# A Swin block and an FFT-gated convolution block on one core: three images in work instead of two, softmax sums on TensorE, norms on ScalarE, and every engine's order rewritten

## The chip, the cores and the metric

The kernel runs on 1 core of one Trainium2 chip. Its time is device time in microseconds (us). Before the change it is 1808.63 us, the median of 3 runs (1806.32 to 1815.72).

## What is computed

The input is `x`, 16 images of 128 channels by 32 x 32 pixels, all in fp32. Each image goes through two blocks in turn.

The first is a Swin block over 16 windows of 8 x 8 tokens, with 8 heads of 16 channels:

```python
t = ln(tok, ln1_g, ln1_b)                      # in windows of 64 tokens
q, k, v = split(t @ qkv_w.T + qkv_b)
attn = softmax(q * 16**-0.5 @ k.T + bias)      # per window and head, 64 x 64
tok = tok + (attn @ v) @ proj_w.T + proj_b
tok = tok + gelu(ln(tok, ln2_g, ln2_b) @ w1.T + b1) @ w2.T + b2
```

The second is a convolution block:

```python
out0 = gelu(conv1x1(x, in_w, in_b))
x_fca = abs(ifft2(fft2(out0) * x_att))         # = |x_att| * |out0|
xs = x_att2 * x_fca                            # x_att, x_att2: per-channel factors from means
x_sca = abs(ifft2(conv(xs, fgm_w1) * fft2(conv(xs, fgm_w2)) * (1 + boost * mask))) * alpha + xs * beta
h_out, v_out = two 7-tap dilated axis convolutions of out0, each then a 3x3 depthwise one
pyr = 3x3 depthwise of four grouped 3x3 convolutions of out0 with dilations 1, 6, 12, 20
edge = sigmoid(3x3 convolution of out0 to one channel)
out = conv1x1(relu(x + c0*(1+edge)*h_out + c1*(1+edge)*v_out + c2*(1-0.3*edge)*pyr + c3*point + c4*x_sca))
```

## The kernel before

Each of the five engines has one instruction stream written out by hand, and semaphores join them. TensorE, VectorE, ScalarE and GpSimd each run `swin_rest(0)` (on GpSimd `swin_only`), then `both(n, i)` fifteen times, with n the image in the convolution block and i = n + 1 the image in the Swin block, and last `conv_only(15)`. In `both` the work of the two images is interleaved by hand. In each stream it has three stretches.

- The front: the input is put in window order (`to_windows`, L1324), turned to tokens by TensorE (`x_transposes`, L473) and copied (`x_copy`). VectorE takes the first norm's statistics and applies the norm with eight `tensor_scalar` (`norm1`, L938, through `normalise`, L929). TensorE turns the result back and makes keys, queries and values (`queries_keys` L486, `v` L497). VectorE adds the bias of the keys (L949), and SyncE spreads them over `k_heads` with eight DMAs (`spread_keys`, L428), for which the first `scores` waits (`kh_dma`). Beside it runs the head of the convolution block of image n: `in_conv` (L602), its gelu (L1407), channel means and factors (L999 to L1026), and the first half of the four dilated convolutions (`pyramid`, L657, matmul at L674).
- Eight slots, one for each pair of windows j. `scores` (L518) goes into bank 2 or 3, VectorE adds the bias (L957) and takes the row maximum (L960), GpSimd subtracts it (`less_max`, L1666), ScalarE takes the exponential (L1382), VectorE sums the rows and inverts the sums (L964, L966), GpSimd widens the inverses (`widen_inverse`, L1677), TensorE turns the exponentials (L529), ScalarE copies them (L1387), and `values` (L540) multiplies them with v. After four pairs each, `spread_inverse` (L551) turns the inverses and VectorE multiplies with them (L972). The spectrum of the convolution block is laid through the slots by `conv_early` and `conv_late` on TensorE and ScalarE, and by `conv_slot` on VectorE, with 9 of the 18 taps of the depthwise convolutions (`taps`, L1088 and L1090). A tap is one VectorE pass over 128 x 1024 values.
- The tail: projection, residual and second norm (`residual_stats` L974, `norm2` L984), the MLP (`mlp`, L565: eight `up` matmuls, eight gelus, two `down` groups), and on VectorE the last 9 taps, then `gate_axes`, `add_magnitude`, `mixture` (L1143 to L1159) and `swin_out` (L988). Then ScalarE's `rectify` and TensorE's `out_conv` (L755) end image n.

GpSimd also makes the two axis convolutions (`axis_conv`, L1684), `resT` (L1660), `mix_pyramid` (L1718) and `square_sum` (L1725). `xs` is kept turned, so that `mirrored` (L1028) reads rows of the image in its inner loop. The sum over the nine shifted edge planes is a matmul with ones (`edge_spread`, L637).

Of the kernel before, what the change touches and what calls it, by code (L numbers as in the profile page):

```python
# [48 lines left out]
RUN = 31 * S1 + SIDE  # L49
# [6 lines left out]
def layout(*entries):  # L56
# [21 lines left out]
    ("even", P), ("odd0", P), ("odd", P), ("idft_h", P), ("high", CH), ("iota", 2))  # L78


def shape_constants():
# [41 lines left out]
    idft = diag(unpack, unpack, unpack, unpack).reshape(P, 4, n)  # L123
    put("idft_h", idft.transpose(0, 2, 1).reshape(P, P))
# [12 lines left out]
    put("iota", np.stack([np.arange(P), np.arange(P) + P], 1))  # L137
    return c.astype(np.float32)


def swin_conv_kernel(nc, x, cols, rows, mats, cons, rel_index, out):
    with ExitStack() as ctx:
# [46 lines left out]
        attn_out = xw  # L189
        xT = sb("xT", CH, C)  # L190
        x1T = xT
# [3 lines left out]
        qC, kC = sb("qC", TOK), sb("kC", TOK)  # L195
        k_heads = sb("k_heads", HEADS, WIN, WT)
# [4 lines left out]
        stats, mv = sb("stats", CH, 6), sb("mv", CH, 2)  # L201
        std, rstd = sb("std", CH), sb("rstd", CH)
        row_max, row_sum, row_inv = sb("row_max", 3, HEADS), sb("row_sum", 3, HEADS), sb("row_inv", PAIRS, HEADS)
        inv_wide = sb("inv_wide", PAIRS, HEADS, HD)
# [9 lines left out]
        fa, fb, fc, fd, xe, xo = (fft[:, k] for k in range(6))  # L214
        hidden = fft[:, 2:6]
# [3 lines left out]
        z_run = sb("z_run", 32 * S1)  # L219
        z_grid = z_run.rearrange("p (h w) -> p h w", w=S1)  # L220
        z_dram = nc.dram_tensor("z_dram", (9, GRID1), F32, kind="Internal")
        axis_part = sb("axis_part", SIDE, SIDE)
# [38 lines left out]
        ln1_std = sem("ln1_std")  # L261
        nT_sb = sem("nT_sb")
# [12 lines left out]
        s_max = sem("s_max")  # L275
        s_sub = sem("s_sub")
        s_exp = sem("s_exp")
        s_inv = sem("s_inv")
        iv_wide = sem("iv_wide")
        iv_ps = sem("iv_ps")  # L280
# [4 lines left out]
        o_sb = sem("o_sb")  # L285
# [3 lines left out]
        ln2_std = sem("ln2_std")  # L289
        n2T_sb = sem("n2T_sb")  # L290
# [25 lines left out]
        eb_ps = sem("eb_ps")  # L316
# [38 lines left out]
        mag_sb = sem("mag_sb")  # L355
        hv_sb = sem("hv_sb")
# [17 lines left out]
        xs_hw = xs.rearrange("p (w h) -> p h w", w=SIDE)  # L374
# [5 lines left out]
        SLOT_TAPS = (0, 0, 0, 2, 4, 4, 5, 7, 9)  # L380
# [3 lines left out]
        def _(sp):  # L384
# [52 lines left out]
            with sp.Fori(0, IMAGES - 2) as n:  # L437
                load(n + 2)
                spread_edge(n)
                spread_keys(n + 1)  # L440
                stack_pyramid(n)
                store(n)
# [11 lines left out]
        def _(pe):  # L454
# [110 lines left out]
            def mlp(i):  # L565
# [25 lines left out]
                for t in range(3):  # L591
                    up(t)
# [1250 lines left out]
```

## Time and profile before

| | |
|---|---|
| median of 3 runs | 1808.63 us |
| the profiled execution | 1805.41 us, its span 1803.6 us |
| span, `both` of one image | 106.6 to 109.7 us, in the mean about 108.3 |
| TensorE, mean granted clock | 0.953 of full speed |
| DMA share | small: 33 GB/s in the mean |

The busy shares of the engines stand in the rows below. An engine's busy share is an average over the three stretches. What the change is worth is read from which engine each stretch waits for. In the rows of the profile, x counts records; every fp32 matmul of the program leaves two, a transpose one. L numbers are lines of the kernel before.

### The profile page before, as it was taken

Reading aid. Unit: us, or ns where it says so; the run is one execution under the profiler, and the core shown is the slowest. Engines: PE = TensorE matmul, PEld = TensorE weight load, DVE = VectorE, ACT = ScalarE, POOL = GpSimd, SP = SyncE. Lnnn points to the kernel's source line nnn. Section 1 sums busy time; section 2 is a strip of 40 time slices with the busy share of each in tenths; the row PEclk is TensorE's granted clock in tenths of the full one; section 3 lists DMA queues with packets and bytes.
Section 4 is the critical chain, followed back from the end, with each engine's and each line's share of the span. In section 5 each row is a group of like instructions: output and inputs, shape, how many; then the busy total and the mean of one; then the engine's idle time right before and its main releaser. Section 6 shows DMA issues by size and latency. Waiting matters only on the chain.

```text
span 1803.6 us, 32142 instructions
## 1 busy us (share of the span) xinstructions
PE 1549.4 (86%) x11664; PEld 906.3 (50%) x11664; DVE 1364.0 (76%) x2455; ACT 864.2 (48%) x1380; POOL 684.9 (38%) x603
## 2 busy tenths in 40 slices
PE   5789899888989889888998988889888898988884
PEld 3346455464555546445463554546455464555542
DVE  4558778687777878788687777868788786778866
ACT  2344545455454544545455454544545545454533
POOL 3244251634416244251534416134251623416151
PEclk9899999999999999999999999999999999999997
DMA  4011020111102011020111102011020201102020
GB/s 147 1 26 41 26 52 1 43 33 37 39 23 53 0 37 39 25 51 0 43 33 37 39 23 53 0 37 39 25 51 0 58 18 37 39 12 53 0 54 12
DMA packets 19618, 60.23 MB, mean 33 GB/s; under 512 B 6228, under 2 KB 6228, under 8 KB 19204
## 3 DMA queue, kind: packets, MB, share of 16 engines
q1 hardware_dynamic: 19588, 59.83, 13.7%
q8 instruction: 18, 0.29, 0.1%
q14 instruction: 12, 0.10, 0.0%
HBM read 14.04 MB, written 9.02 MB: 13 GB/s over the span
## 4 chain that ended last, share of the span: by engine, by line
DVE 39%; PE 25%; DVEq 16%; issue 7%; ACT 6%; SPq 4%; DMA 3%; ACTq 1%; POOL 0%; POOLq 0%
DVE hv L1090 16%; DVEq L959 7%; DVE nT L929 5%; PE bank L647 5%; PE bank L674 4%; SPq L428 4%; DVE row_max L960 4%; DVEq L965 3%; PE bank L467 3%; PE bank L518 3%; PE bank L489 2%; DMA k_heads<-kC 2%; PE bank L755 2%; DVE score L957 2%; PE bank L577 1%
## 5 line engine op out<-in xcount | busy, mean ns | idle before, releaser
L674 PE MATMUL bank<-act,mats_sb 128*32 128x512 f32 (+11 forms) x2112 | 267.1, 475 | 1.4 <-DVE xs L1026 1.4
L1666 POOL TENSOR_TENSOR score<-score,row_max 128x512 f32<-128x512 f32 x128 | 133.4, 1042 | 306.7 <-DVE row_max L960 305.1
L1350 ACT ACTIVATE fft<-bank 128x512 f32<-128x512 f32 x224 | 168.9, 807 | 125.7 <-PE bank L467 111.8
L1090 DVE SCALAR_TENSOR_TENSOR hv<-hor,mix,hv 128x1024 f32<-128x1024 f32 x128 | 193.8, 1514 | 10.7
L467 PE MATMUL bank<-cons_sb,fft 128*128 128x128 f32 x1280 | 185.4, 306 | 11.8 <-DVE fft L1117 11.8
L1090 DVE SCALAR_TENSOR_TENSOR hv<-ver,mix,hv 128x1024 f32<-128x1024 f32 x144 | 186.9, 1298 | 11.0
L1382 ACT ACTIVATE score<-score 128x512 f32<-128x512 f32 x128 | 80.8, 631 | 225.8 <-POOL score L1666 225.8
L467 PEld LDWEIGHTS bank<-cons_sb,fft 128*128 128x128 f32 x1280 | 172.7, 217 | 31.4 <-DVE fft L1117 17.0
L1677 POOL COPY inv_wide<-row_inv 128x128 f32<-128x128 f32 x128 | 91.8, 717 | 206.7 <-DVE row_inv L966 206.7
L674 PEld LDWEIGHTS bank<-act,mats_sb 128*32 128x32 f32 x2112 | 117.5, 109 | 99.6 <-issue 81.5
L1696 POOL TENSOR_SCALAR hor<-act,cols_sb 128x1024 f32<-128x1024 f32 x16 | 18.0, 1125 | 391.6 <-ACT act L1407 391.6
L518 PE MATMUL bank<-k_heads,qC 128*64 128x512 f32 x512 | 136.1, 621 | 31.8 <-DMA k_heads<-kC 31.8
L577 PE MATMUL bank<-nC,mats_sb 128*128 128x512 f32 x256 | 127.4, 621 | 38.9 <-ACT nC L1350 23.4
L957 DVE TENSOR_TENSOR score<-bank,rel_bias 128x512 f32<-128x512 f32 x128 | 87.2, 681 | 76.3 <-PE bank L518 76.2
L1387 ACT ACTIVATE probT<-bank 128x512 f32<-128x512 f32 x128 | 77.7, 607 | 101.6 <-PE bank L529 101.3
L1706 POOL TENSOR_SCALAR axis_part<-act,cols_sb 128x320 f32<-128x320 f32 (+1 forms) x128 | 109.4, 855 | 22.5 <-issue 22.5
L587 PE MATMUL bank<-fft,mats_sb 128*128 128x512 f32 x256 | 115.2, 593 | 0.0
L1400 ACT ACTIVATE fft<-bank,fold_b 128x512 f32<-128x512 f32 x128 | 79.2, 689 | 68.5 <-PE bank L577 68.5
L929 DVE TENSOR_SCALAR nT<-xT,mv,rstd 128x128 f32<-128x128 f32 x256 | 104.8, 491 | 3.8
L1708 POOL TENSOR_TENSOR ver<-ver,axis_part 128x320 f32<-128x320 f32 (+1 forms) x64 | 100.8, 1575 | 9.4
L960 DVE TENSOR_REDUCE row_max<-score 128x8 f32<-128x512 f32 x128 | 87.8, 686 | 11.6
L577 PEld LDWEIGHTS bank<-nC,mats_sb 128*128 128x128 f32 x256 | 45.1, 191 | 98.2 <-issue 34.4
(180 smaller groups left out, 2903.9 us busy)
## 6 DMA issues: line engine op xcount, KB each, us to landing
pyr_stack<-pyr SPq DMA_DIRECT2D x192, 144.2 KB, 3.1
x_in<-x_dram SPq DMA_DIRECT2D x16, 512.0 KB, 3.5
k_heads<-kC SPq DMA_DIRECT2D x128, 64.0 KB, 2.4
out_dram<-y_out SPq DMA_DIRECT2D x16, 512.0 KB, 2.8
k_heads<-rel_dram SPq DMA_DIRECT2D x2, 1024.0 KB, 13.0
mats_sb<-mats_dram SPq DMA_DIRECT2D x1, 1978.5 KB, 7.4
z_dram<-z_sb SPq DMA_DIRECT2D x32, 19.1 KB
z_run<-z_dram SPq DMA_DIRECT2D x16, 38.2 KB
```

What stands on the lines that cost most here:

```text
L467: last = pe.matmul(dst[:, c * P:(c + 1) * P], src[:, at:at + P], rhs, start=True, stop=True)
L518: last = pe.matmul(bank[2 + j % 2][64 * e:64 * e + 64, :], qC[:, w * WT:(w + 1) * WT], k_heads[:, :, w], start=True, stop=True)
L577: pe.matmul(bank[b][:], w_up[:, f * P:(f + 1) * P], nC[:, HALF * k:HALF * k + HALF], start=True, stop=True).then_inc(up_ps, 1)
L587: last = pe.matmul(bank[b][:], w_down[:, f * P:(f + 1) * P], hidden[:, f, HALF * k:HALF * k + HALF], start=False, stop=(f == FC - 1))
L674: last = pe.matmul(grids[32 * d:32 * d + 32, y0 - 16 * k:y1 - 16 * k, x0:x1], w_pyr[:, d, t], act[:, y0 + dy:y1 + dy, x0 + dx:x1 + dx], st ...
L929: last = dve.tensor_scalar(nT[:, c], source[:, c], mv[:, c, 0:1], rstd[:, c:c + 1], ALU.subtract, ALU.mult)
L957: dve.tensor_tensor(score[:, j % 3].rearrange("p h k -> p (h k)"), bank[2 + j % 2][:], rel_bias[:], ALU.add).then_inc(s_biased, 1)
L959: dve.drain()
L960: dve.tensor_reduce(row_max[:, j % 3], score[:, j % 3], AX.X, ALU.max).then_inc(s_max, 1)
L1090: last = dve.scalar_tensor_tensor(hv[:], src, mix[:, a, k:k + 1], hv[:], ALU.mult, ALU.add)
L1350: return act_.activation(dst, src, ACT.Copy)
L1666: pool.tensor_tensor(score[:, j % 3], score[:, j % 3], row_max[:, j % 3].unsqueeze(2).broadcast_to([P, HEADS, WT]), ALU.subtract)\
```

## The change

In words, part by part:

1. Three images are in work. `both(n, i, f, late)` convolves image n, does attention and MLP of i = n + 1, and does the front of f = n + 2 (turns, norm 1, keys, queries, values) inside the slots 6 and 7 and inside the MLP of i. The end of image late = n - 1 (`gate_axes`, `add_magnitude`, `mixture`, `rectify`, `out_conv`) is moved to the start of `both`.
2. Softmax: `row_sums`, `widen_inverse` and `spread_inverse` go. `values` adds four matmuls for each pair of windows with a constant `pair`, which sum the exponentials; VectorE inverts 128 x 128 sums from PSUM and multiplies, once for each pair. The subtraction of the maximum moves from GpSimd to VectorE. All scores go through bank 2, one at a time.
3. Norms: VectorE computes 1/std and -mean/std, ScalarE applies them, eight activations for each norm. The keys' bias, `swin_out` and the first tap move from VectorE to ScalarE.
4. Spectrum: `xs` is kept in natural order and unscaled; the factor goes into `w1_scaled` and `w2_scaled` (128 x 128). `mirrored` makes only the 17 distinct rows, and `part_products` multiplies them in 64 matmuls with 32-column weights in place of 16 with 128.
5. `mix_pyramid` and `square_sum` move from GpSimd to VectorE. The edge sum leaves TensorE: three DMAs bring nine planes in rows, VectorE sums them, ScalarE takes the tanh of 32 x 32 values, and two DMAs through DRAM spread it over 128 partitions.
6. The taps: one on ScalarE in slot 2, one on VectorE in slot 6, one after `norm2(i, 0)`, two after the statistics of image f, thirteen at the very end. On TensorE, `conv_early` stands ahead of `scores` in a slot, and `pyramid_conv` is moved behind the slots.

The core of the diff (TensorE, VectorE, ScalarE; a line of "..." marks what is left out):

```diff
             def values(i, j):
                 pe.wait_ge(pT_sb, 8 * i + j + 1)
-                if j == 4:
-                    pe.wait_ge(o_sb, 2 * i + 1)
+                if j >= 2:
+                    pe.wait_ge(o_scaled, 8 * i + j - 1)
...
+                for g in range(HP):
+                    last = pe.matmul(ps[32 * g:32 * g + 32, P:2 * P], con("pair"),
+                                     probT[:, j % 2, g], start=True, stop=True)
                 last.then_inc(o_ps, 1)
...
+            def part_products(dst, parts, k):
+                for c in range(4):
+                    for q in range(4):
+                        a, r = divmod(4 * (4 * k + c) + q, 2)
+                        at = SIDE * (r if a == 0 else a + 1)
+                        last = pe.matmul(dst[32 * q:32 * q + 32, c * P:(c + 1) * P], parts[:, at:at + SIDE],
+                                         w1_scaled[:], start=True, stop=True)
+                return last
...
+            def both(n, i, f, late):
+                scores(i, 0)
+                in_conv(n, i + 1)
+                scores(i, 1)
                 edge_products(n)
                 pyramid(n, 0, range(0, 2))
                 gap_products(n)
+                pyramid(n, 0, range(2, 6))
                 mid_products(n)
+                pyramid(n, 0, range(6, 9))
                 for j in range(PAIRS):
+                    conv_early(n, j)
                     if j + 2 < PAIRS:
                         scores(i, j + 2)
                     prob_transposes(i, j)
+                    if j == 0 and late is not None:
+                        pe.wait_ge(z_copied, n + 1)
+                        pe.wait_ge(xs_sb, 2 * n + 1)
+                        out_conv(late)
                     conv_late(n, j)
+                    if j == 6 and f is not None:
+                        next_turns(i, f, 0)
+                    elif j == 7:
+                        project(i, 0, f)
                     values(i, j)
+                if f is not None:
+                    next_turns(i, f, 1)
                 last_odd(n)
                 project(i, 1)
+                pyramid_conv(n, 0)
                 n2_transposes(i, 0)
+                pyramid_conv(n, 1)
+                n2_transposes(i, 1)
+                mlp(i, n, f)
...
+                for t in range(6):
+                    up(i, t)
+                down(i, 0)
+                half_of(turn, 0)
+                half_of(turn, 1)
+                up(i, 6)
+                half_of(key, 0)
+                half_of(key, 1)
+                up(i, 7)
+                half_of(query, 0)
+                half_of(query, 1)
+                half_of(value, 0)
+                half_of(value, 1)
+                down(i, 1)
...
+            def scale_values(i, j):
+                dve.wait_ge(o_ps, 8 * i + j + 1)
+                ps = bank[(1, 3)[j % 2]]
+                dve.reciprocal(inverse[:, j % 2], ps[:, P:2 * P])
+                dve.drain()
+                dve.tensor_tensor(attn_out[:, P * j:P * j + P], ps[:, 0:P], inverse[:, j % 2], ALU.mult)\
+                   .then_inc(o_scaled, 1)
...
+            def both(n, i, f, late):
+                if late is not None:
+                    gate_axes(late)
+                    add_magnitude(late)
+                bias_max(i, 0)
                 gap(n)
+                bias_max(i, 1)
                 attention_vectors(n)
+                if late is not None:
+                    mixture(late)
                 scaled_input(n)
                 even_part(n)
                 route_logits(n)
                 for j in range(PAIRS):
+                    if j in (4, 5):
+                        conv_slot(n, j)
+                    if j > 0:
+                        scale_values(i, j - 1)
...
+                if f is not None:
+                    norm1_stats(f, 0)
+                scale_values(i, 7)
                 residual_stats(i, 0)
                 norm2(i, 0)
+                taps(n, range(SLOT_TAPS[PAIRS], SLOT_TAPS[PAIRS + 1]))
                 residual_stats(i, 1)
                 norm2(i, 1)
+                square_sum(n)
+                if f is not None:
+                    norm1_stats(f, 1)
+                taps(n, range(SLOT_TAPS[PAIRS + 1], SLOT_TAPS[PAIRS + 2]))
+                if f is not None:
+                    norm1(f)
+                gate_pyramid(n)
+                mix_pyramid(n)
+                taps(n, range(SLOT_TAPS[PAIRS + 2], 18))
```

Here `SLOT_TAPS` is (1, 1, 1, 1, 1, 1, 1, 2, 2, 3, 5), where it was (0, 0, 0, 2, 4, 4, 5, 7, 9).

## Rows read from the trace of the kernel before

**Rows 1.** The page: busy time by engine, dilated convolutions, keys' DMAs (last: us to landing).
```profile
PE 1549.4 (86%) x11664; PEld 906.3 (50%) x11664; DVE 1364.0 (76%) x2455; ACT 864.2 (48%) x1380; POOL 684.9 (38%) x603
L674 PE MATMUL bank<-act,mats_sb 128*32 128x512 f32 (+11 forms) x2112 | 267.1, 475 | 1.4 <-DVE xs L1026 1.4
...
k_heads<-kC SPq DMA_DIRECT2D x128, 64.0 KB, 2.4
```
**Rows 2.** Busy time by stretch: three images, the first Swin part, the last convolution.
```profile
core 0: us, PE busy (x) PEld busy (x) DVE busy (x) ACT busy (x) POOL busy (x), PEclk, DMA share, GB/s
751.90:1076.10 324.20, 285.98 (x2167) 167.26 (x2166) 252.97 (x453) 161.01 (x260) 125.82 (x111) 0.96 0.14 32
...
38.30:99.30 61.00, 43.42 (x334) 23.47 (x333) 25.94 (x64) 26.33 (x44) 10.32 (x16) 0.86 0.06 10
1724.50:1803.60 79.10, 49.16 (x361) 29.76 (x359) 52.89 (x58) 27.04 (x38) 29.03 (x20) 0.85 0.14 37
```
**Rows 3.** The same view in steps of 5 us, where the granted clock is low.
```profile
875.00:880.00 5.00, 5.00 (x13) 1.88 (x13) 3.51 (x5) 0.78 (x2) 4.68 (x4) 0.59 0.15 22
...
920.00:925.00 5.00, 4.68 (x19) 3.66 (x19) 4.65 (x7) 3.64 (x5) 2.15 (x2) 0.50 0.00 0
```
**Rows 4.** TensorE in order of time: start, us, line, x [idle before <-releaser].
```profile
873.34 3.78 PE L489 MATMUL bank<-nC,mats_sb 128*128 128x512 f32 x4
...
886.61 4.42 PE L674 MATMUL bank<-act,mats_sb 128*32 128x512 f32 x40
...
899.62 0.43 PE L540 MATMUL bank<-probT,v_pair 128*32 128x64 f32 x16
899.98 1.08 PE L518 MATMUL bank<-k_heads,qC 128*64 128x512 f32 x4
...
904.22 1.09 PE L459 MATMUL bank<-cons_sb,fft 128*128 128x128 f32 x8 [0.74 <-ACT fft L1350]
...
958.40 1.88 PE L577 MATMUL bank<-nC,mats_sb 128*128 128x512 f32 x4
```
**Rows 5.** Groups of TensorE by line and form, 751.9 to 1076.1 us.
```profile
L467 PE MATMUL bank<-mats_sb,fft 128*128 128x128 f32 x96 | 12.2, 280 | 3.8 <-DVE fft L1099 3.8
L551 PE MATMUL bank<-cons_sb,inv_wide 128*128 128x128 f32 x48 | 6.6, 281 | 0.0
L637 PE MATMUL bank<-z_run,ones 9*128 9x512 f32 x12 | 6.2, 634 | 3.0 <-DVE fft L1113 3.0
```
**Rows 6.** Groups of VectorE, the same three images.
```profile
L929 DVE TENSOR_SCALAR nT<-xT,mv,rstd 128x128 f32<-128x128 f32 x48 | 19.5, 473 | 0.7
L957 DVE TENSOR_TENSOR score<-bank,rel_bias 128x512 f32<-128x512 f32 x24 | 16.4, 681 | 11.8 <-PE bank L518 11.8
L964 DVE TENSOR_REDUCE row_sum<-score 128x8 f32<-128x512 f32 x24 | 16.2, 677 | 0.0
L1032 DVE TENSOR_TENSOR fft<-xs 128x930 f32<-128x930 f32 x6 | 14.1, 2342 | 0.3
```
**Rows 7.** Two lines of VectorE reciprocals over the run: ns least/median/most; 4, 8 values.
```profile
L926 DVE RECIPROCAL rstd<-std x48: 165/178/205, 23.4 to 1702.8; 128x4 f32<-128x4 f32 x32, 128x8 f32<-128x8 f32 x16
L966 DVE RECIPROCAL row_inv<-row_sum x128: 202/203/205, 51.7 to 1691.1; 128x8 f32<-128x8 f32 x128
```
**Rows 8.** VectorE in order of time, one image's tail.
```profile
936.90 4.42 DVE L1090 SCALAR_TENSOR_TENSOR hv<-hor,mix,hv 128x1024 f32<-128x1024 f32 x2
...
945.16 0.69 DVE L978 TENSOR_TENSOR xT<-bank,resT 128x512 f32<-128x512 f32 x1
...
946.89 0.38 DVE L921 BATCH_NORM_AGGREGATE mv<-stats 128x2 f32<-128x6 f32 x4
...
949.10 12.16 DVE L1090 SCALAR_TENSOR_TENSOR hv<-ver,mix,hv 128x1024 f32<-128x1024 f32 x9
```
**Rows 9.** GpSimd in order of time, beside the first row of Rows 8.
```profile
936.52 2.36 POOL L1718 TENSOR_TENSOR py<-py,xm 128x1024 f32<-128x1024 f32 x1
```
**Rows 10.** SyncE's queue in order of time: one image's spreading of the keys.
```profile
877.94 5.02 SPq L428 DMA_DIRECT2D k_heads<-kC  x8
```
**Rows 11.** A ScalarE group of small activations, the same three images.
```profile
L1329 ACT ACTIVATE xw<-x_in 128x256 f32<-128x256 f32 x14 | 4.7, 404 | 0.0
```

More of the change, by code:

```diff
@@ L508, in scores, with v @@
+            def v(i, k, b):
+                wv = w_qkv[:, 2 * C:3 * C].rearrange("p (g e d) -> p e g d", g=HP, e=2)
+                for w in range(8):
+                    t = nC1[:, (8 * k + w) * WT:(8 * k + w + 1) * WT]
+                    for e in range(2):
+                        last = pe.matmul(bank[b][64 * e:64 * e + 64, w * 64:w * 64 + 64], t, wv[:, e],
+                                         start=True, stop=True)
+                last.then_inc(v_ps, 1)
             def scores(i, j):
@@ new lines, in down @@
+            def down(i, k):
+                b = (0, 3)[k]
+                pe.wait_ge(up_sb, 8 * i + 4 + 4 * k)
+                for c in range(4):
+                    pe.matmul(bank[b][:, c * P:(c + 1) * P], x1T[:, 4 * k + c], ident, is_transpose=True,
+                              start=(c == 0), stop=False)
+                for f in range(FC):
+                    last = pe.matmul(bank[b][:], w_down[:, f * P:(f + 1) * P],
+                                     hidden[:, f, HALF * k:HALF * k + HALF], start=False, stop=(f == FC - 1))
+                last.then_inc(down_ps, 1)
@@ L760, in conv_early @@
                 if j == 1:
-                    pyramid(n, 1, range(6, 9))
+                    pyramid(n, 1, range(4, 9))
                 elif j == 2:
@@ L848, in conv_only @@
                 mid_products(n)
-                pyramid(n, 1, range(0, 5))
+                pe.wait_ge(z_copied, n + 1)
+                pe.wait_ge(xs_sb, 2 * n + 1)
+                out_conv(n - 1)
                 for j in range(PAIRS):
@@ L853, in conv_only @@
                 last_odd(n)
+                pyramid_conv(n, 0)
+                pyramid_conv(n, 1)
+                for k in range(2):
+                    pe.wait_ge(py_sb, 2 * n + k + 1)
                 out_conv(n)
@@ L1235, in conv_only @@
                     conv_slot(n, j)
-                    if j == 3:
-                        r_even_bias(n)
+                    taps(n, range(SLOT_TAPS[j], SLOT_TAPS[j + 1]))
                 taps(n, range(SLOT_TAPS[PAIRS], 18))
+                square_sum(n)
+                gate_pyramid(n)
+                mix_pyramid(n)
                 gate_axes(n)
```

828 lines of the change are left out of this document (401 added, 427 removed).

## The prediction, made before the changed kernel ran

> **What bounds the kernel now.** I read the busy shares first. TensorE is busy 86% of the span, VectorE 76%, the others under half [rows 1]. Over three images in the steady state that is 95.3 us of TensorE and 84.3 us of VectorE in a period of about 108.1 us [rows 2]. So neither is the bound alone: 12.8 us of each period TensorE has nothing to do. Then the clock: in two places of each image it falls to the lower of its two levels (1.2 of 2.4 GHz), after stretches in which TensorE had waited for the norms and for VectorE's half of the spectrum [rows 3]. Four records of 512 columns then take 3.78 us, against 1.88 us at full clock [rows 4]. Over both places I put this at about 5 us of the 95.3. Last the order of time: the tail has nine taps in a row on VectorE, 12.16 us [rows 8], and only behind them come the passes that free `rectify` and `out_conv`. The next image's front then runs as one long chain (turn, statistics, norm, turn, keys, DMA), in which the keys' DMAs alone take 5.02 us of issue and 2.4 us of landing [rows 1, 10].
>
> So the period is a ring through several engines. What the change brings is the shortest ring that is left, not the sum of what it removes.
>
> **TensorE's work.** Removed: `edge_spread`, 6.2 us in three images, 2.1 each, and `spread_inverse`, 6.6, 2.2 each [rows 5]. For what is added I need the price of matmuls with 32-column weights. The 40 records at 886.61 are steps 0 to 4 of `pyramid`, each step four matmuls into four partition groups. By the shapes in the code their longest members have 512, 496, 512, 496, 496 columns, 2512 together, for 4.42 us [rows 4]: 1.7 ns for each column of the longest, the other three free. `values` agrees: two steps of 64 columns, 0.36 us from its start to the next one's [rows 4]. The sums by `pair` are one such step of 128 columns for each of 8 pairs: 8 x 0.21 = 1.7 us. Were the four one after another, it would be 0.43 each, 3.5 us. `part_products` is 16 steps of 128 columns, 3.5 us, in place of 96 records in three images, 12.2 us, 4.1 each [rows 5]; one after another it would be 14. The sum is -2.1 - 2.2 + 1.7 - 0.6 = -3.2 us, up to +9 if nothing runs side by side. I take -3.2, the nearest rows being of the same form. With the clock kept, TensorE needs about 87 us.
>
> **VectorE's work.** Removed for each image: applying the norms, 19.5/3 = 6.5 us; row sums 5.4 [rows 6] and their inverses 8 x 0.2 = 1.6 [rows 7]; keys' bias, `scale_values`, first tap and `swin_out`, about 5.4 by the same kind of passes. `mirrored` handles 465 values where it had 930, at 2342 ns twice [rows 6]: -2.4. `xs` unscaled and in natural order: about -2. In sum -23. Added: subtracting the maximum, a pass like L957's at 0.68 us [rows 6], 8 x 0.69 = 5.5; `mix_pyramid` and `square_sum` 2.5; the edge sum, small vectors and inverses 1.2; and 8 times a reciprocal of 128 x 128 and a product. No row shows a reciprocal of that width. Four values take 165 to 178 ns, eight 203 [rows 7], so 6.3 to 9.5 ns a value: 0.96 to 1.34 us, and 0.28 if the width cost as little as in a sum. I take 1.1, with 0.3 for the product 8 x 1.4 = 11.2. VectorE ends near 84.3 - 23 + 20.4 = 82 us, hardly less than before, with about 5 us of drains between the passes. The gain can't come from VectorE being relieved.
>
> The Trainium skill (VectorE: DVE Perf Modes, First, the fixed hardware budget) says that Reciprocal repeats its divide step 8 times. That is the same direction as the slope in the rows; it gives no other sum.
>
> **The ring after the change.** I call D the moment when VectorE starts the bias of `scores(i, 0)`, V the end of `values(i, 7)` on TensorE.
>
> D to V is TensorE's: since all scores share bank 2, `scores(i, 1)` waits for that first bias, 0.8 us. Then at full clock: seven `scores` at 1.0, 7.1; eight groups of four turns at 0.5 (eight turns: 1.09 [rows 4]), 4.0; `pyramid` 267.1/16 = 16.7 [rows 1]; `values` with the sums 8 x 0.57 = 4.6; five products of the spectrum at 16 records x 0.127 = 2.0, the columns 2.0 and both `part_products`, 15.7; the turns of the spectrum, of x and `project`, 4.0; the late `out_conv` 1.9; edge and vector products 1.5. Together 55.5, so V at D + 56.3. To this come waits for ScalarE's copies, 0.74 us at a time [rows 4], since `conv_early` now stands ahead of the `scores` that covered them, and some low clock after D: I add 4.2. V at D + 60.5.
>
> V to the next D is VectorE's: the last `scale_values` with its wait 1.7; `residual_stats` twice, 945.16 to the end of the aggregates at 947.27, 2.1 each [rows 8], 4.2; the two roots and inverses 1.9; `square_sum` 1.3; statistics of image f 1.4; inverses 0.4; `gate_pyramid` and `mix_pyramid` 2.9; and 1 + 2 + 13 taps at 12.16/9 = 1.35 [rows 8], 21.6; then `gate_axes` and `add_magnitude` of the late image 2.7. Together 38.1. TensorE needs less in the same stretch: last products and `pyramid_conv` 8.7, the wait for the second norm 2, eight `up` 7.2 and two `down` 8.0 (0.9 us a matmul of 512 columns [rows 4]), the front of f 6.5, together about 33; the keys' DMAs are hidden behind queries, values and `down(1)`. The ScalarE part (sixteen norm activations at under 0.4 us [rows 11], keys, `swin_out`) lies within it.
>
> To this comes what GpSimd takes from VectorE. At 936.90 two taps take 4.42 us, not 2.7, while a GpSimd pass of 2.36 us runs [rows 8, 9]: VectorE stands until that pass is over. In the new tail `resT` falls among VectorE's passes (1.2), and `axis_conv` starts with `gate_axes` and `add_magnitude` (1.7): 41.0. The period is 60.5 + 41.0 = 101.5 us, against 108.3.
>
> **The total.** The first Swin part ends at 38.3 + 61.0 = 99.3 us [rows 2]; it gets the front of image 1, and loses GpSimd's steps: the first D at 104. Fifteen periods, 1522.5, less 5 because the last has no image f. From the last D to the end, now 79.1 us for the whole of `conv_only` [rows 2]: less 7 (half mirrors, one tap, GpSimd's two slow passes), plus 2.6 for the late image's passes: 74.5. The sum is 104 + 1522.5 - 5 + 74.5 = 1696 us of span. The profiled execution lies 1.8 above its span, and the median of the runs 3.2 above the profiled execution: 1700 us.
>
> **The rivals.**
> 1. The waits, the low clock and GpSimd's share come out at almost nothing. The ring is then 56.3 + 38.1 = 94.4, with one or two us left 96: 104 + 1440 + 69.5 = 1614 us (69.5 is 74.5 - 5), 1619 measured. For it: the new order has far fewer chains of several engines, and TensorE alone needs 87. Against it: VectorE's tail must leave TensorE idle for some 5 us each image, and such gaps cost clock before.
> 2. The gain is given back in the slots. One bank for `scores` and `conv_early` at the head make each slot wait for a copy and a bias: 8 slots x 0.74 us [rows 4] more than I have, period 107.4, 1785 to 1790 us. Against it: VectorE is ahead of TensorE in the slots by about 5 us in my timeline.
> 3. Slower: GpSimd and VectorE stand in each other's way on the ring. GpSimd's `axis_conv` and `resT` (125.8/3 = 41.9 us [rows 2] less its steps for the softmax and its two passes, about 19) now come in one block behind D, where VectorE has about 16 passes that GpSimd can hold up. I have priced these at 9 us in all. If each pays what the tap at 936.90 paid, 4.42 - 2.7 = 1.7 us [rows 8], it is 27, 18 more; about 5 is slack, so the period is 114.5: 104 + 1717.5 + 69.5 = 1891, 1896 measured. It decides from 12 us more than I have. For it: every pass of this stretch stands ahead of what TensorE waits for (`mid_products`, `out_conv`). Against it: GpSimd ran under VectorE before as well, and its group L929 there lost only part of its time [rows 6].
>
> The Trainium skill (SBUF — State Buffer, Who interferes with whom) says that a VectorE instruction with two SBUF inputs and a GpSimd one that reads SBUF exclude each other for their whole length. By that rule rival 3 has its mechanism, and the trace agrees at 936.90; how often they meet, it doesn't say.
>
> That the change doesn't do what it says is in rival 2: the front is moved, but its time comes back as waits.
>
> **How the numbers follow.** Forecast 0.64 (ring 98 to 105.5, 1645 to 1760 us), rival 1 0.14, rival 2 0.12, rival 3 0.10. The range takes in the forecast, the upper half of rival 1 and rival 2's lower part: 1625 to 1785, leaving out about 0.2. The reciprocal's bounds move the period by under 2 us (one lies in the tail, eight use up slack), the packed matmuls' upper bound by 12. Two measurements of this kernel differ by up to about 0.5%, 9 us: faster by more 0.86, within it 0.04, slower 0.10.
>
> **What would show it.** Period by the stores near 101.5 us. VectorE's thirteen taps in a row, some 17.6 us, and TensorE waiting 3 to 6 us at `scores(i, 1)` for VectorE: right. TensorE waiting for the keys' DMA instead: the tail is not VectorE's. The reciprocal of 128 x 128 near 1.1 us; the `pair` group near 0.2 us a pair; `part_products` near 1.75 us a call. Taps and subtractions well over 1.28 and 0.7 us in the first 25 us behind D, with TensorE idle at `mid_products`: rival 3. Idle ahead of each slot's first group: rival 2. It is all wrong if TensorE is never idle ahead of `scores(i, 1)`: then my ring is not the one that closes last.

## The result and the profile after

The changed kernel takes 1600.93 us, the median of 4 runs (1598.29 to 1607.63), beside 1812.18 us for the kernel before on the same chip. The ratio is 0.884, with a 95% interval from 0.880 to 0.888: 11.6% faster. The forecast was 1700 us and its range ended at 1625; the time lies 24 us below it, and 18 us below the 1619 of rival 1. The sign was right, the size was not.

The page of the kernel after, its span, its busy shares and its row of the TensorE clock in 40 slices:

```profile
span 1600.2 us, 36298 instructions
PE 1453.8 (91%) x13904; PEld 843.6 (53%) x13904; DVE 1287.5 (80%) x2311; ACT 942.7 (59%) x1685; POOL 376.6 (24%) x315
PEclk9889999999999999999999999999999999999987
```

Three images of its steady state, as [rows 2] shows them for the kernel before (stretch, its length, the busy time of each engine with its records, granted clock, DMA share, GB/s):

```profile
783.60:1067.40 283.80, 268.03 (x2595) 156.10 (x2587) 240.12 (x427) 175.31 (x316) 68.81 (x58) 0.99 0.17 42
```

For each image TensorE is busy 89.3 us (95.3 before), VectorE 80.0 (84.3), GpSimd 22.9 (41.9). TensorE's idle time has gone from 12.8 us to 5.3. The stores of the images lie 94.5 us apart in the mean of 13 intervals, where the kernel before had 108.1 (14 intervals) and the forecast was 101.5. So neither engine was relieved by much. Of the 13.5 us between the two windows, 7.5 is idle time of TensorE that is gone, 6.0 its busy time.

TensorE from one D to the stretch behind it. Columns: start, duration, engine, line, operation, output and inputs, records, and in brackets the idle time before it and who ended it.

```profile
862.07 1.08 PE L530 MATMUL bank<-k_heads,qC 128*64 128x512 f32 x4 [2.87 <-DVE score L1013]
863.94 3.52 PE L703 MATMUL bank<-act,mats_sb 128*32 128x512 f32 x12
867.77 3.42 PE L703 MATMUL bank<-act,mats_sb 128*32 128x480 f32 x26
875.90 1.88 PE L795 MATMUL bank<-fft,mats_sb 128*128 128x512 f32 x4
...
894.37 0.40 PE L557 MATMUL bank<-probT,cons_sb 128*32 128x128 f32 x8
894.59 1.93 PE L734 MATMUL bank<-w_scaled,fft 128*32 128x128 f32 x64
...
918.80 0.40 PE L557 MATMUL bank<-probT,cons_sb 128*32 128x128 f32 x8
...
951.37 1.08 PE L530 MATMUL bank<-k_heads,qC 128*64 128x512 f32 x4
952.38 1.98 PE L652 MATMUL bank<-xm,mats_sb 128*128 128x512 f32 x4
957.23 1.08 PE L530 MATMUL bank<-k_heads,qC 128*64 128x512 f32 x4 [2.87 <-DVE score L1013]
```

The first record is `scores(i, 1)`, and it waits 2.87 us for VectorE's first bias, as does the last, one image later. `scores(i, 0)` and `in_conv` of that next image (951.37, 952.38) are done well before: the keys' DMAs, which had 5.02 us of issue on the path [rows 10], are out of it. V is 919.20, the end of the last `pair` sums. An image without low clock behind the same wait, and the granted clock at both places (columns as above):

```profile
768.63 1.08 PE L530 MATMUL bank<-k_heads,qC 128*64 128x512 f32 x4 [2.87 <-DVE score L1013]
780.76 1.88 PE L795 MATMUL bank<-fft,mats_sb 128*128 128x512 f32 x4
```

```profile
768.60:773.60 5.00, 4.97 (x45) 2.08 (x48) 4.30 (x10) 2.75 (x4) 4.37 (x5) 1.00 0.04 8
862.10:867.10 5.00, 5.00 (x22) 1.17 (x22) 3.58 (x6) 1.96 (x3) 4.37 (x5) 0.66 0.04 7
```

VectorE from V to the next D:

```profile
919.27 0.96 DVE L1026 RECIPROCAL inverse<-bank 128x128 f32<-128x128 f32 x1 [0.88 <-PE bank L557]
920.51 0.68 DVE L1036 TENSOR_TENSOR x1T<-bank,resT 128x512 f32<-128x512 f32 x1
930.42 2.65 DVE L1144 SCALAR_TENSOR_TENSOR hv<-hor,mix,hv 128x1024 f32<-128x1024 f32 x2
936.19 5.36 DVE L1144 SCALAR_TENSOR_TENSOR hv<-hor,mix,hv 128x1024 f32<-128x1024 f32 x4
941.62 12.16 DVE L1144 SCALAR_TENSOR_TENSOR hv<-ver,mix,hv 128x1024 f32<-128x1024 f32 x9
955.29 1.28 DVE L1215 SCALAR_TENSOR_TENSOR hv<-fft,mix,hv 128x1024 f32<-128x1024 f32 x1
956.50 0.68 DVE L1013 TENSOR_TENSOR score<-bank,rel_bias 128x512 f32<-128x512 f32 x1
```

But for two waits of 0.37 and 0.36 us for ScalarE's roots it works on to the next bias at 956.50. So the ring of the forecast is there: V to D on VectorE is 37.3 us, in the other images 37.2 to 37.5 (forecast 41.0). D to V on TensorE is 861.34 to 919.20, 57.9 us, in this image (forecast 60.5). The image at 768.63 has the same wait and takes 56.2, since the clock stays at its upper level there. Of the 14 images from D = 201.90 on, seven have the full clock and 56.2 us, seven the low one and 57.7 to 57.9, one of these 59.1. In the mean over all fifteen, D to V is 57.0, and the period from D to D is 94.3. The sum of the bare terms had been 94.4.

### The profile page after: what moved, and what is told of

Same layout as the page of the kernel before. It is cut to its first block, busy times and chain, and to the rows that moved or that the text cites. A ratio compares the mean times of both kernels' runs of the same rounds, so it can differ in the third digit from the quotient of the medians.

```text
span 1600.2 us, 36298 instructions
## 1 busy us (share of the span) xinstructions
PE 1453.8 (91%) x13904; PEld 843.6 (53%) x13904; DVE 1287.5 (80%) x2311; ACT 942.7 (59%) x1685; POOL 376.6 (24%) x315
## 4 chain that ended last, share of the span: by engine, by line
DVE 39%; PE 28%; DVEq 16%; ACT 10%; issue 6%; DMA 1%; SPq 0%; ACTq 0%
DVE hv L1144 17%; PE bank L703 15%; ACT fft L1444 4%; DVEq L1015 4%; PE bank L530 3%; DVE row_max L1016 3%; DVEq L1027 3%; DVE stats L984 2%; PE bank L795 2%; ACT probT L1487 2%; DVEq L1039 2%; DVE score L1018 2%; DVEq L985 2%; DVE score L1013 1%; PE bank L673 1%
## 5 line engine op out<-in xcount | busy, mean ns | idle before, releaser
L703 PE MATMUL bank<-act,mats_sb 128*32 128x512 f32 (+11 forms) x2112 | 280.0, 492 | 0.0
L1806 POOL TENSOR_TENSOR resT<-qC,proj_shift 128x1024 f32<-128x1024 f32 x16 | 38.0, 2377 | 622.6 <-DVE x1T L1036 618.0
L703 PEld LDWEIGHTS bank<-act,mats_sb 128*32 128x32 f32 x2112 | 121.6, 113 | 104.7 <-issue 83.0
L1144 DVE SCALAR_TENSOR_TENSOR hv<-hor,mix,hv 128x1024 f32<-128x1024 f32 x128 | 164.4, 1284 | 10.6
L1444 ACT ACTIVATE fft<-bank 128x512 f32<-128x512 f32 x224 | 165.4, 810 | 12.8 <-PE bank L489 11.6
L489 PE MATMUL bank<-cons_sb,fft 128*128 128x128 f32 x1280 | 162.0, 280 | 7.8 <-DVE fft L1177 7.2
L1013 DVE TENSOR_TENSOR score<-bank,rel_bias 128x512 f32<-128x512 f32 x128 | 87.4, 682 | 96.9 <-PE bank L530 96.9
L489 PEld LDWEIGHTS bank<-cons_sb,fft 128*128 128x128 f32 x1280 | 148.8, 192 | 20.8 <-DVE fft L1177 10.8
L1026 DVE RECIPROCAL inverse<-bank 128x128 f32<-128x128 f32 x128 | 122.0, 953 | 44.2 <-PE bank L557 44.2
L1018 DVE TENSOR_TENSOR score<-score,row_max 128x512 f32<-128x512 f32 x128 | 98.8, 772 | 10.0 <-issue 0.5
L541 PEld LDWEIGHTS bank<-cons_sb,score 128*128 128x128 f32 x512 | 55.7, 142 | 79.1 <-issue 66.1
L1016 DVE TENSOR_REDUCE row_max<-score 128x8 f32<-128x512 f32 x128 | 87.8, 686 | 11.7
L1838 POOL TENSOR_TENSOR hor<-hor,axis_part 128x320 f32<-128x320 f32 (+1 forms) x64 | 94.3, 1473 | 9.4 <-issue 0.2
L683 PE MATMUL bank<-pyr_stack,mats_sb 96*32 96x512 f32 x768 | 88.9, 596 | 0.0
```

Source lines behind the costliest of these rows:

```text
L489: last = pe.matmul(dst[:, c * P:(c + 1) * P], src[:, at:at + P], rhs, start=True, stop=True)
L703: last = pe.matmul(grids[32 * d:32 * d + 32, y0 - 16 * k:y1 - 16 * k, x0:x1], w_pyr[:, d, t], act[:, y0 + dy:y1 + dy, x0 + dx:x1 + dx], st ...
L1016: dve.tensor_reduce(row_max[:, j % 3], score[:, j % 3], AX.X, ALU.max)
L1018: dve.tensor_tensor(score[:, j % 3], score[:, j % 3], row_max[:, j % 3].unsqueeze(2).broadcast_to([P, HEADS, WT]), ALU.subtract)\
L1026: dve.reciprocal(inverse[:, j % 2], ps[:, P:2 * P])
L1144: last = dve.scalar_tensor_tensor(hv[:], src, mix[:, a, k:k + 1], hv[:], ALU.mult, ALU.add)
```

## The experiments

My theory, once the trace was read: the ring D, V, D is what sets the period; its bare sum was right, and the two allowances on top were too large (4.2 us for copies and low clock between D and V, 2.9 for GpSimd). The runs were made on several chips, on which the kernel before took 1811 to 1815 us; a difference of a few us counts only where the traces show it too, from D to D. Rivals: VectorE as a whole sets the time, so that any pass taken from it counts in full; or GpSimd's passes set it; or the gain comes from single parts (the norms on ScalarE) that would have brought it in the old order too.

**Two taps fewer in the tail.**

```diff
-                taps(n, range(SLOT_TAPS[PAIRS + 2], 18))
+                taps(n, range(7, 18))
```

> The changed kernel with two of the thirteen taps at the end of VectorE's tail left out (taps 5 and 6, so the output lacks them). Ring theory: the period is TensorE from D to V and VectorE from V to the next D, and TensorE stands 2.87 us ahead of scores(i, 1) in each image. Two taps are 2.7 us, so each of 15 periods falls by 2.7 us, from 94.5 to 91.8, the whole from 1601 to about 1560 us, and the wait ahead of scores(i, 1) shrinks to 0.2 us. Rival TensorE (busy 94% of the period, so it is the bound and VectorE is beside it): no change, 1595 to 1601. Rival VectorE's sum (busy 80 of 94.5): also 1560, told apart by the run with five taps less.

Measured: 1547.41 us (ratio 0.854, 0.850 to 0.859), 53 us less for 40 us of passes. More comes back than is taken out. Two images in a row:

```profile
927.13 0.68 DVE L1013 TENSOR_TENSOR score<-bank,rel_bias 128x512 f32<-128x512 f32 x1
1017.88 0.69 DVE L1013 TENSOR_TENSOR score<-bank,rel_bias 128x512 f32<-128x512 f32 x1
```

The last `pair` sums of this image start at 982.90 and take 0.40. So D to V is 56.2 us and V to D 34.6. The tail is shorter by the taps, 2.7, in every image, about 40 us in all. TensorE waits no more than 0.17 us at `scores(i, 1)`, the granted clock behind it is 1.00 in every image, and D to V is 56.2 in 11 of 15. That takes 1.7 us, once 3.0, from the seven images that had low clock behind the wait, 13 us together. 40 and 13 make up the 53. I had expected 1560: the clock was not in it. My own sum for D to V without allowance had been 56.3.

**Five taps fewer.**

```diff
-                taps(n, range(SLOT_TAPS[PAIRS + 2], 18))
+                taps(n, range(10, 18))
```

> The changed kernel with five taps of the thirteen left out (6.75 us). Ring theory: the ring closes through TensorE's own tail as soon as 2.9 us are gone, since scores(i, 1) stands behind in_conv there; period 91.6, total about 1557 us, nearly the same as with two taps less. Rival VectorE's sum: 6.75 x 15 = 101 us less, 1500. Rival TensorE: no change.

Measured: 1540.50 us (0.851, 0.846 to 0.855). Three more taps, 4 us an image, bring 7 us in all. VectorE alone would have brought 60 more; that rival is dead. Now VectorE waits at D for TensorE:

```profile
924.76 0.69 DVE L1013 TENSOR_TENSOR score<-bank,rel_bias 128x512 f32<-128x512 f32 x1 [2.71 <-PE bank L530]
1015.29 0.69 DVE L1013 TENSOR_TENSOR score<-bank,rel_bias 128x512 f32<-128x512 f32 x1 [2.72 <-PE bank L530]
```

The period is 90.5 us, TensorE's floor with this order. The expected 1557 was again 17 us too high.

**Two taps made twice.**

```diff
-                taps(n, range(SLOT_TAPS[PAIRS + 2], 18))
+                taps(n, (5, 6, *range(5, 18)))
```

> The changed kernel with two taps of the tail done twice (the output has them twice). Ring theory: period 94.5 + 2.7 = 97.2, total 1601 + 40 = 1641 us, the wait ahead of scores(i, 1) 5.6 us in place of 2.87; some more low clock behind it may add up to 1 us a period (1656). Rival TensorE: up to 2.9 us a period are free, 1601.

Measured: 1667.88 us (0.921, 0.916 to 0.925), 67 us more for 40 us of passes; I had expected up to 55.

```profile
899.60 1.97 PE L530 MATMUL bank<-k_heads,qC 128*64 128x512 f32 x4 [6.26 <-DVE score L1013]
998.62 1.98 PE L530 MATMUL bank<-k_heads,qC 128*64 128x512 f32 x4 [6.27 <-DVE score L1013]
...
996.00 1.97 DVE L1215 SCALAR_TENSOR_TENSOR hv<-fft,mix,hv 128x1024 f32<-128x1024 f32 x1
```

The period is 99.0. The wait has grown from 2.87 to 6.26 us, and `scores(i, 1)` takes 1.97 us where it took 1.08: the low clock now follows in every image but the first (0.50 to 0.56 in the 5 us behind the wait), and D to V is 58.3 where the mean was 57.0. The magnitude pass ahead of D takes 1.97 instead of 1.28, as it starts at 996.00 while GpSimd's first `axis_conv` pass, 2.20 us from 994.69, still runs. So of 4.7 us a period 2.7 are the taps, 1.3 the clock and 0.7 GpSimd's.

**Almost no axis convolution on GpSimd.**

```diff
-            OFFSETS = [0] + [AXIS_DIL * (t - mid) for t in range(AXIS_TAPS)
-                             if t != mid and abs(AXIS_DIL * (t - mid)) < SIDE]
+            OFFSETS = [0]
```

> The changed kernel with only the centre tap of both axis convolutions on GpSimd (the others left out, the output lacks them): GpSimd works 2.3 us there instead of about 20. Ring theory: VectorE loses about 5 us to GpSimd within the first 22 us behind D, but in a stretch where it later waits 3.7 us for scores(i, 3), so the period stays within 0.5 us, total 1593 to 1601. Contention theory (my rival 3 at a smaller size: that the hold-ups are on the ring): 3 to 5 us a period less, 1526 to 1556 us.

Measured: 1604.03 us (0.886, 0.880 to 0.892), the same as with all of it. The page of the profile counts GpSimd busy 99.4 us instead of 376.6, and nothing came of it:

```profile
961.90 1.08 PE L530 MATMUL bank<-k_heads,qC 128*64 128x512 f32 x4 [2.87 <-DVE score L1013]
```

The same wait of 2.87 us. What GpSimd takes from VectorE behind D falls into slack. Rival 3 has no room left.

**The biases ahead of the late image's passes.**

```diff
-                if late is not None:
-                    gate_axes(late)
-                    add_magnitude(late)
                 bias_max(i, 0)
                 gap(n)
+                if late is not None:
+                    gate_axes(late)
+                    add_magnitude(late)
                 bias_max(i, 1)
                 attention_vectors(n)
```

> The changed kernel with VectorE's order at the start of an image turned: bias and maximum of scores(i, 0) and the channel mean first, then gate_axes and add_magnitude of the late image (2.7 us). Nothing is left out. Ring theory: scores(i, 1) starts 2.7 us earlier, the wait of 2.87 us ahead of it falls to about 0.2, period 94.5 - 2.7 = 91.8, total 1601 - 38 = 1563 us. Rival: the two passes then stand ahead of the channel factors, TensorE waits at mid_products instead, and the period stays at 94 to 94.5 (1594 to 1601).

Measured: 1588.19 us (0.876, 0.874 to 0.878), 12.7 us less, where I had expected 38. The wait did not go, it moved:

```profile
863.75 0.38 PE L665 MATMUL bank<-vec,mats_sb 128*128 128x1 f32 x2 [1.94 <-DVE vec L1067]
956.45 0.38 PE L665 MATMUL bank<-vec,mats_sb 128*128 128x1 f32 x2 [1.95 <-DVE vec L1067]
```

TensorE now waits 1.94 us at `mid_products`, because the passes stand ahead of `attention_vectors`. V to D is 34.5 us, 2.8 less, but D to V is 58.2, and in five of 13 periods 59.8 to 60.8: there the granted clock from 10.7 us behind D to V is 0.97, in the others 1.00. My ring had one point of contact; there are two close together. The expectation failed on that, and on the clock.

**Both norms back on VectorE.**

```diff
+                dve.wait_ge(nT_ps, 2 * i)
                 invert(mv1, std1, rstd1, shift1, ln1_inv, slice(0, CH))
+                apply_norm(nT1, xT, mv1, rstd1, range(CH), nT_sb)
...
+                dve.wait_ge(n2T_ps, 2 * i)
                 invert(mv2, std2, rstd2, shift2, ln2_inv, slice(4 * k, 4 * k + 4))
+                apply_norm(nT, x1T, mv2, rstd2, range(4 * k, 4 * k + 4), n2T_sb)
```

`normalise1` and `normalise2` go from ScalarE.

> The changed kernel with both norms applied by VectorE again, sixteen passes over 128 x 128, and not by ScalarE: this undoes one part of the change. Before, four of them took 1.1 us without GpSimd beside them. Ring theory: all sixteen lie between V and the next D, 4.5 us more, period 99, total 1601 + 67 = 1668 us; the second norm reaches TensorE a little earlier, which helps nothing. Rival TensorE: 2.9 us of it free, about 1 us a period, 1616 us.

Measured: 1704.92 us (0.941, 0.938 to 0.943), 104 us more: half of the whole gain hangs on this part. The sixteen passes of one image in three groups, the D behind them, and the wait one image later (L993 and L1023 are lines of this kernel, the norm and the bias):

```profile
883.66 1.11 DVE L993 TENSOR_SCALAR nT<-x1T,mv,rstd 128x128 f32<-128x128 f32 x4
889.41 1.12 DVE L993 TENSOR_SCALAR nT<-x1T,mv,rstd 128x128 f32<-128x128 f32 x4
896.09 2.14 DVE L993 TENSOR_SCALAR nT<-qC,mv,rstd 128x128 f32<-128x128 f32 x8
922.08 0.68 DVE L1023 TENSOR_TENSOR score<-bank,rel_bias 128x512 f32<-128x512 f32 x1
...
1024.74 1.97 PE L530 MATMUL bank<-k_heads,qC 128*64 128x512 f32 x4 [5.88 <-DVE score L1023]
```

V is 879.4, so V to D is 42.7 us, 5.4 more than after the change: 4.4 are the passes, and 0.7 is the magnitude pass ahead of D, which takes 1.97 instead of 1.28 behind GpSimd's first, as with two taps more. D to V is 57.7 to 59.4, in the mean 58.6 instead of 57.0: with a wait of 5.88 us the low clock comes in every image but the first (0.70 to 0.85 in the 10 us behind it). The period is 101.3 in the mean. I had expected 1668: the 37 us on top are this clock and the 0.9 us by which V to D passed my 4.5.

**The same part alone, in the kernel before.** VectorE makes 1/std and -mean/std, ScalarE applies both norms, everything else as before:

```diff
             def norm1(i):
                 dve.wait_ge(ln1_std, i + 1)
-                dve.wait_ge(xT_sb, 2 * i + 2)
-                dve.wait_ge(n2T_ps, 2 * i)
-                normalise(xT, nT_sb)
+                invert(rstd1, shift1, ln1_inv)
...
                 deviation1(i)
+                normalise1(i)
                 n_copy(i)
```

> The kernel before with one part of the change alone: VectorE makes 1/std and -mean/std, ScalarE applies both norms. In the old order the norm stands on the chain to the keys: eight activations of 0.40 us (3.2) in place of passes that took 2.2 to 4.3, and one more hand-over; the second norm costs TensorE some 0.5 us twice, and VectorE's tail begins 2.2 us earlier. In sum between +1 and -2 us an image: 1805 us (1780 to 1825). Rival: what counts is the work that VectorE gives up, 5 to 6 us an image, as undoing the same part after the change cost 6.5 us and more: then 1720 us or less.

Measured: 1825.33 us, 1.008 of the kernel before (1.005 to 1.011): a little slower, at the upper end of what I expected. The rival's 1720 is refuted: the part is worth nothing by itself. TensorE at the first matmuls of the MLP, first in this kernel, then in the kernel before:

```profile
956.02 2.81 PE L581 MATMUL bank<-nC,mats_sb 128*128 128x512 f32 x6 [1.86 <-ACT nC L1366]
```

```profile
946.68 2.81 PE L577 MATMUL bank<-nC,mats_sb 128*128 128x512 f32 x6 [0.78 <-ACT nC L1350]
```

Over the whole run TensorE waits 40.9 us at this line for `nC`, against 23.4 in the kernel before. In the old order TensorE waits for the norm itself, and ScalarE is slower at it. In the new order the norm lies beside other work, and what counts is VectorE's length.

**Two taps fewer in the kernel before.**

```diff
-                taps(n, range(SLOT_TAPS[PAIRS], 18))
+                taps(n, range(SLOT_TAPS[PAIRS], 16))
```

The edit stands in `both` and in `conv_only`.

> The kernel before, with the last two of the eighteen taps left out (part of the computation is missing). Did the kernel before hang on VectorE's tail? In its trace TensorE waits 1.35 us at the output matmul for the end of that tail, while the MLP had ended just before. If that wait is all, the 2.7 us of the two taps bring 1.4 us an image and a little clock: 1785 us (1775 to 1795). Rival: VectorE's tail stands on the ring in full, as it does after the change, where two taps brought 3.6 us an image: then 1750 to 1765 us.

Measured: 1788.32 us (0.988, 0.985 to 0.991), 22.7 us less, as expected. The same edit brought 53 us after the change. What ended TensorE's idle time ahead of `out_conv` (L755), in the kernel before and in this one (us, times):

```profile
  ACT fft L1521: 37.3, 14
```

```profile
  ACT fft L1521: 17.0, 1
```

In the kernel before, 19.74 of the 37.3 us stand in the last image, the other 13 waits are 1.35 us each. With two taps fewer those 13 are gone. So before the change VectorE's tail stood on the path for 1.4 us an image at most; what stood behind it was the path.

**Two passes back on GpSimd.** `mix_pyramid` and `square_sum`, each with its waits, as in the kernel before:

```diff
-                square_sum(n)
                 if f is not None:
                     norm1_stats(f, 1)
...
                 gate_pyramid(n)
-                mix_pyramid(n)
```

> The changed kernel with mix_pyramid and square_sum on GpSimd again, each one pass of 2.35 us over 128 x 1024, instead of 1.23 on VectorE: this undoes another part. Both lie between V and the next D. Theory that the two engines exclude each other for whole passes: VectorE saves 2.5 us and loses up to 2.35 at each of the two (it stood that long at 936.90 before), so the period is 94.5 + 0 to 2.2, total 1601 to 1635 us. Theory that GpSimd's time is free: period 92, total 1565 us.

Measured: 1611.67 us (0.889, 0.886 to 0.892), 11 us more, although VectorE has 2.5 us less to do in each image. The interval touches that of the changed kernel (0.880 to 0.888), but the traces differ too, 95.1 us from D to D against 94.3. First GpSimd's two passes, then VectorE's taps beside them:

```profile
935.75 2.35 POOL L1844 TENSOR_TENSOR fft<-fft 128x1024 f32<-128x1024 f32 x1
942.59 3.25 POOL L1837 TENSOR_TENSOR py<-py,xm 128x1024 f32<-128x1024 f32 x1 [4.49 <-DVE py L1191]
...
937.14 3.40 DVE L1144 SCALAR_TENSOR_TENSOR hv<-hor,mix,hv 128x1024 f32<-128x1024 f32 x2
942.34 7.30 DVE L1144 SCALAR_TENSOR_TENSOR hv<-hor,mix,hv 128x1024 f32<-128x1024 f32 x4
```

Two taps take 3.40 us instead of 2.65, four take 7.30 instead of 5.36: 2.7 us of waiting for 2.5 us of work handed over. V to D is 37.55 us instead of 37.3, so nothing is saved, and 4 us in all are lost. The rest of the 11 is TensorE's clock: behind the wait, here 2.49 us, it is low in 12 of 14 images, where it was in 7, and D to V is 57.7 to 57.9 in them. Why it is so in more of them I can't say. A GpSimd pass of this kind runs in VectorE's time when VectorE has two-input passes to make. The Trainium skill (SBUF — State Buffer, Who interferes with whom) says that such pairs exclude each other; here the trace agrees, and the statistics at 935.73, which have one input, are not held up.

**A version built from these: three taps early.** The slots have slack on VectorE (it waits 3.67 us for `scores(3)` at 886.83), the tail has none. The first tap goes to slot 0 on ScalarE, two more stand in slot 1 ahead of the bias of `scores(3)`:

```diff
-        SLOT_TAPS = (1, 1, 1, 1, 1, 1, 1, 2, 2, 3, 5)
+        SLOT_TAPS = (3, 3, 3, 3, 3, 3, 3, 4, 4, 5, 7)
...
+                    if j == 1:
+                        taps(n, range(1, 3))
                     if j + 2 < PAIRS:
                         bias_max(i, j + 2)
```

> The changed kernel with the first tap (ScalarE) in slot 0 and taps 1 and 2 (VectorE) in slot 1 ahead of the bias of scores(i, 3), where VectorE waits 3.7 us for TensorE; eleven taps in the tail instead of thirteen. Nothing is left out. Ring theory: the same work, 2.7 us of it moved from the ring into slack: period 91.8 to 92.3, total 1560 to 1568 us, as with two taps left out. Theory that VectorE's sum counts: no change, 1595 to 1601.

Measured: 1547.47 us (4 runs; 0.854, 0.852 to 0.856): nothing left out, and as fast as with two taps fewer. TensorE at D, and four images of it:

```profile
928.92 1.08 PE L530 MATMUL bank<-k_heads,qC 128*64 128x512 f32 x4 [0.16 <-DVE score L1013]
930.40 2.22 PE L703 MATMUL bank<-act,mats_sb 128*32 128x512 f32 x12
941.05 1.88 PE L795 MATMUL bank<-fft,mats_sb 128*128 128x512 f32 x4
```

```profile
783.00:1147.00 364.00, 353.11 (x3456) 207.27 (x3459) 323.97 (x569) 233.29 (x421) 94.44 (x76) 1.00 0.18 43
```

The wait is 0.16 us, the clock full, TensorE busy 97%. From this `scores(i, 1)` to `out_conv` it is 12.13 us (928.92 to 941.05); after the change it was 13.83 (862.07 to 875.90), the same instructions and no wait of TensorE between them. The image at 768.63 took 12.13 as well, with the wait. So it is the low clock that costs 1.7 us, in the images that have it; here none has it. The run lies 13 us below the lower end of what I had expected; that share of the clock, 13 us, was not counted in it.

**And the last image.** On top of it, for `conv_only` alone (shown beside the changed kernel):

```diff
                 gap_products(n)
-                pyramid(n, 0, range(0, 9))
+                pyramid(n, 0, range(0, 4))
                 mid_products(n)
+                pyramid(n, 0, range(4, 9))
...
                 for j in range(PAIRS):
                     conv_slot(n, j)
-                    taps(n, range(SLOT_TAPS[j], SLOT_TAPS[j + 1]))
-                taps(n, range(SLOT_TAPS[PAIRS], 18))
+                    if j == 2:
+                        taps(n, range(1, 9))
+                taps(n, range(9, 18))
```

> The early taps of the run before, and two changes for the last image alone: TensorE makes the vector products behind step 4 of the pyramid instead of behind step 9, and VectorE makes the taps 1 to 8 right behind the third slot's work instead of behind the sixth's. In the run before, VectorE stood idle there for 6.97 us (for the vector products) and for 3.02 us (for the first product of the spectrum), while TensorE waited 15.79 us for VectorE at its end. If VectorE's work sets the end of the last image, nearly all of the 10 us comes back: 1538 us (1534 to 1542). Rival: TensorE's spectrum sets it, being started no earlier; then 1544 to 1548, no change.

Measured: 1541.12 us (4 runs; 0.852, 0.849 to 0.854), 6.3 us less than the run before it; that is 14.9% below the kernel before, and the fastest of all that compute everything. It was another chip, and the two intervals overlap, but from the last D of `both` to the end the traces have 156.2 us against 162.0. TensorE's idle time ahead of the last `out_conv` went from 15.79 us to 7.46:

```profile
1504.66 3.30 PE L734 MATMUL bank<-w_scaled,fft 128*32 128x128 f32 x64 [1.97 <-DVE fft L1153]
1530.77 3.75 PE L795 MATMUL bank<-fft,mats_sb 128*128 128x512 f32 x4 [7.46 <-ACT fft L1654]
```

I had counted on nearly all of 10 us. VectorE still waits 2.35 us for the vector products, and the group at 1504.66 now takes 3.30 us instead of 1.95, behind a wait.

## Why the prediction was wrong, point by point

- *What bounds the kernel, and the ring after the change.* Right. It is TensorE from D to V and VectorE from V to D, with `scores(i, 1)` waiting 2.87 us (said: 3 to 6, so just below). Taking time from VectorE's tail moves the period, taking it from GpSimd does not. The old kernel had no such ring: two taps are worth 22.7 us there and 53 here.
- *The bare sums.* Right, and that they hit within 0.1 us is partly luck. D to V was 56.3 us, measured 56.2 wherever the clock is full, 57.0 in the mean. V to D was 38.1; measured 37.3, of which about 0.4 is GpSimd's. So one sum was 0.7 short and the other 0.8 long, and 94.4 stands against 94.3.
- *The allowance of 4.2 us between D and V.* This step failed. It was put down in one line, "waits for ScalarE's copies, 0.74 us at a time" and some low clock, with no count of places. Measured is 57.0 - 56.3 = 0.7 us in the mean: nothing in one half of the images, 1.7 in the other. Between `scores(i, 1)` and V TensorE waits twice, 0.52 us for a copy of ScalarE's and 0.48 for VectorE, and the bare sum absorbed both; the rest is the low clock, 0.81 and 0.84 from 860 to 870 us.
- *The allowance of 2.9 us for GpSimd.* This step failed too. I had charged `resT` with 1.2 and the start of `axis_conv` with 1.7, by the tap of 4.42 us [rows 8]. After the change `resT` runs from 925.55, beside statistics and small vectors, and costs 0.4: L993 (there -mean/std) takes 0.55 us, not 0.16. At D it was GpSimd that gave way: its first pass takes 2.09 us instead of 1.12, VectorE's two passes their usual 1.23 and 1.28. VectorE's pass had started 0.20 us before it. In the kernel with two taps more GpSimd's pass was the one under way, and VectorE's took 1.97 us. The 9 us that rival 3 says were priced in all stand nowhere in the forecast's sum; it has these 2.9.
- *The size.* 15 periods came out 104.7 us shorter than forecast, and the ends 8.9 longer (the first D at 109.1, said 104; the last D to the end 78.3, said 74.5). In the first Swin part, with no convolution beside it, the second and third `scores` each wait 0.79 us for the one bank, at low clock, and are 2.8 us apart; the later slots wait 0.69 to 1.70 us for ScalarE's copy. That is the mechanism of rival 2, but in one image of sixteen.
- *The rivals.* Rival 1 was the true case; it had a chance of 0.14. The argument held against it, that gaps of TensorE cost clock, is true, but the price is 1.7 us, in half of the images. Its period of 96 had another 1.6 us for safety. The fault is the same in both: a sum of some twenty terms, most of them from rows, was trusted less than two lumps on top. Rival 2 did not happen in the steady state, rival 3 not at all.
- *Terms of TensorE.* The `pair` sums start 0.22 us ahead of `part_products` (894.37 to 894.59; said 0.21) and 0.33 ahead of groups with 128-column weights (918.80 to 919.13). `part_products` takes 1.77 and 1.86 us from its start to that of the next group (said 1.75). So 32-column steps do run side by side. TensorE's own time fell by 6.0 us an image; 3.2 had been forecast from the work. The other 2.8 I put to the clock, which is 0.99 instead of 0.96 in the steady state; no run separates the two.
- *Terms of VectorE.* The reciprocal of 128 x 128 takes 0.953 us (said 1.1, bounds 0.96 and 1.34), just under the lower bound. The thirteen taps take 5.36 and 12.16 us, 17.5 (said 17.6). VectorE's busy time is 80.0 us (said 82).

```profile
L1026 DVE RECIPROCAL inverse<-bank 128x128 f32<-128x128 f32 x24 | 22.9, 953 | 7.0 <-PE bank L557 7.0
```

- *"The gain can't come from VectorE being relieved."* Half right. VectorE is hardly relieved in sum, and the norm's move alone brings nothing in the old order. In the new order the same move is worth 104 us, since it stands on the part of VectorE that the ring goes through. The other parts (three images in work, the sums by `pair`, the spectrum, the edge sum) were not undone one by one; what each is worth stays open.

## What to carry to other kernels

Sum the ring from rows, term by term, and test the sum. An allowance on top needs a count and a price as well, or it is only a wish to be safe. Read more than one image before a wait is given a price: here the same wait had a cost in one half of them. What a part is worth depends on the order around it: the norms on ScalarE cost 14 us in the old order and saved 104 in the new one. When an engine's tail closes the ring, move its work to where it has slack, and do so until the other engine no longer waits, for a wait can cost more than its length.

## What the runs showed of the hardware

- A wait of TensorE for 2.87 us was followed by a granted clock of 0.66 in the next 5 us in some images (862.10 to 867.10) and of 1.00 in others (768.60 to 773.60), seven and seven of 14; the low clock cost 1.7 us, in one image 3.0. With a wait of 0.16 the clock stayed at 1.00 in all, with 6.2 to 6.3 (once 5.0) it was 0.50 to 0.56 in all. So taking out 40 us of VectorE's time gained 53.
- When VectorE's two-input passes and GpSimd's pass over 128 x 1024 values meet, either may pay. GpSimd paid 1.0 us at D after the change, where VectorE's pass had started 0.20 us earlier; VectorE paid 0.7 at the same place in the kernel with two taps more, where GpSimd's pass was under way.
- A reciprocal of 128 x 128 values from PSUM takes 953 ns, 7.4 ns for each value of a partition, where passes over 512 values (L1013, L1016) take 0.68 us, 1.3 ns each. The Trainium skill (VectorE: DVE Perf Modes, First, the fixed hardware budget) has the divide repeated 8 times; the ratio here is 5.5.
